# Attention weights exchanged through DRAM instead of turned by TensorE, each pair's reads issued directly behind its own writes

## The reference

```python
def _L1_cond_ref(x, attn_bias, mask, g_in, null_attn_bias, null_kv, Wq, Wkv, Wo, g_out):
    B, N, DIM, H, DH = 8, 256, 256, 16, 64
    xn = layernorm(x, g_in)
    q = (xn @ Wq).reshape(b, n, H, DH).transpose(0, 2, 1, 3) * scale
    k, v = (kv[..., :DH], kv[..., DH:])            # kv = xn @ Wkv, one key head for all 16
    k = jnp.concatenate([nk, k], axis=1)           # one null key ahead of the 256
    v = jnp.concatenate([nv, v], axis=1)
    sim = jnp.einsum('bhid,bjd->bhij', q, k) + bias
    sim = jnp.where(causal_mask, neg, sim)
    sim = jnp.where(mask_p[:, None, None, :], sim, neg)
    attn = jax.nn.softmax(sim, axis=-1)
    out = jnp.einsum('bhij,bjd->bhid', attn, v)
    return layernorm(out.reshape(b, n, INNER) @ Wo, g_out)
```

## Time and profile before

| | |
|---|---|
| median of the runs | 843.15 us (842.95 to 844.2, 3 runs) |
| span of the profiled execution, first to last instruction | 793.7 us |
| what lies around the span, median less span | 49.45 us |
| attention: first transposes of weights to last Wo product | 345.4 to about 657 us of the span |
| PE busy over the span | 748.7 us, 94% |
| DVE / ACT / POOL busy | 453.7 / 381.9 / 422.4 us |

### The profile page before, as it was taken

The page is one execution under the profiler, slowest core; times in us unless marked ns, Lnnn a source line. Parts: engine busy times, 40 slices in busy tenths (PEclk is TensorE's granted clock), DMA queues, the critical chain, the costliest instruction groups (busy, mean ns, idle before and its releaser), DMA issues. The chain is left out here.

```text
span 793.7 us, 16690 instructions
## 1 busy us (share of the span) xinstructions
PE 748.7 (94%) x4993; PEld 595.9 (75%) x4994; DVE 453.7 (57%) x1647; ACT 381.9 (48%) x1094; POOL 422.4 (53%) x506
## 2 busy tenths in 40 slices
PE   8889999769999999989999999999999988899998
PEld 4479966549999999867777777777777754699965
DVE  0824475672232323356666787778878787256557
ACT  3556612242222222166666565656666651777611
POOL 1077327525554852274656668686868356056640
PEclk9999999759999999999999999999999999999999
DMA  9636635429897773395000000000000001356547
GB/s 323 279 108 191 137 118 160 126 81 342 309 329 273 223 231 121 107 401 174 28 1 28 2 28 29 28 29 28 29 1 29 1 29 63 102 160 177 153 149 236
DMA packets 57022, 106.36 MB, mean 134 GB/s; under 512 B 8816, under 2 KB 42864, under 8 KB 55792
## 3 DMA queue, kind: packets, MB, share of 16 engines
q1 hardware_dynamic: 40368, 55.96, 20.9%
q0 software_dynamic: 10944, 30.03, 12.5%
q10 hardware_dynamic: 5632, 19.41, 7.2%
HBM read 78.31 MB, written 27.07 MB: 133 GB/s over the span
## 5 line engine op out<-in xcount | busy, mean ns | idle before, releaser
L2135 POOL TENSOR_TENSOR work<-work,region_ac 128x386 f32<-128x386 f32 x128 | 120.3, 945 | 67.2 <-DVE work L1797 32.7
L1683 ACT ACTIVATE work<-work 128x129 f32<-128x129 f32 (+1 forms) x256 | 114.0, 449 | 5.8 <-DVE work L1797 5.8
L1797 DVE CUSTOM_DVE_ANT_0 work<-psH,work 128x129 f32<-128x129 f32 (+1 forms) x256 | 78.8, 345 | 2.6 <-PE psH L1482 2.6
L1690 ACT COPY work<-psHT 128x384 f32<-128x384 f32 x64 | 30.6, 479 | 86.4 <-PE psHT L1492 86.4
L1355 POOL DMA_INDIRECT d_pairs<-work,home x47 | 46.1, 981 | 42.8 <-DVE home_f L1107 27.4
L1463 PE MATMUL psY<-work,region_ac 128*128 128x256 f32 x256 | 66.9, 384 | 0.5 <-ACT work L1677 0.5
L1516 PE MATMUL psM<-region_ac,work 128*128 128x256 f32 x256 | 66.0, 380 | 0.0
L1025 ACT ACTIVATE work<-work 128x512 f32<-128x512 f32 x39 | 24.6, 630 | 86.0 <-DVE work L1044 86.0
L1344 POOL DMA_INDIRECT b_pairs<-work,home x39 | 38.0, 975 | 49.8 <-DVE work L1051 46.8
L1336 POOL DMA_INDIRECT work<-in_x,inv x39 | 37.0, 949 | 47.0 <-DVE inv L1264 35.5
L848 PE MATMUL psH<-work,region_bd 128*128 128x128 f32 x472 | 59.2, 280 | 2.0 <-ACT region_bd L747 1.1
(11 more groups left out here) (368 smaller groups left out, 1694.6 us busy)
## 6 DMA issues: line engine op xcount, KB each, us to landing
region_bd<-in_b_w ACTq DMA_DIRECT2D x37, 512.0 KB, 5.4
work<-d_rows SPq DMA_DIRECT2D x47, 132.0 KB, 2.2
a_slots<-work SPq DMA_DIRECT2D x19, 256.0 KB, 2.9
region_bd<-in_b_w SPq DMA_DIRECT2D x1, 4096.0 KB, 15.3
work<-b_pairs SPq DMA_DIRECT2D x16, 256.0 KB, 3.1
region_bd<-in_d_w SPq DMA_DIRECT2D x1, 4096.0 KB, 13.2
work<-d_pairs SPq DMA_DIRECT2D x16, 256.0 KB, 4.3
d_rows<-region_bd SPq DMA_DIRECT2D x1, 2112.0 KB, 28.5
```

The source lines that it names most:

```text
L1683: nc.scalar.activation(c_p[:, o, a:z], c_sc[:, o, a:z], ACT.Exp, scale=-1.0, bias=c_min[:, o, i:i + 1], accum_out=c_sum[:, j % 2, o, i:i + ...
L1797: last = nc.vector.tensor_tensor_reduce(c_sc[:, o, a:z], psH[:, o, a:z], c_bm[:, 2 * (j % 2) + o, a:z], 1.0, -LOWEST, ALU.add, ALU.min, c_ ...
L2135: pool.tensor_tensor(c_bm[:, 2 * (j % 2) + o, :], c_mp, c_bias[:, 2 * j + o, :], ALU.subtract).then_inc(C.bm_ready, 1)
```

## The change

PE turns nothing any more. For each pair, DVE turns the weights in 32x32 blocks (`dve_blocks`, one instruction for each head, `c_p` to `c_x1`). SP writes the 384 KB of blocks to a DRAM scratch (`sp_store_blocks`), writes the 4 reciprocals of each partition to another as 512 single elements, and then, in `sp_load_blocks` of the same pair, waits for both writes to land and reads the blocks back in the order in which they make up the turned weights (`c_x2`), and the reciprocals twice, spread over 64 partitions each (`c_over`). SP does this pair after pair in one unrolled loop of 64. The sum of a pair and its product with Wo now come three pairs later (`LAG = 3`) instead of one. `c_x1` and `c_x2` have two slots, `c_over` three, the DRAM scratch four. Scores alternate between the two PSUM tensors `psH` and `psHT`. The keys, the bias and the mask are stored in an order that fits the blocks. `c_x1`, `c_x2`, `c_over` and the values lie where the biases `d_b2` of the last stage were loaded, so these come after the attention; the other weights of the last stage come one piece for each pair from ACT's queue (`act_load_d`), the 4 MB `d_w13` stays on SP ahead of the first pair, and the tiles of `sp_pairs` for later batches are issued by ACT (`act_load_pairs`).

```diff
--- before.py
+++ after.py
...
@@ -26,6 +26,9 @@
 HEADS, DH = 16, 64
 QT = SEQ // P
 KEYS0, KEYS1 = 1 + P, 1 + SEQ
+BLOCK = QT * P + P
+ORDER = (1, 0)
+LAG = 3
 KEYS = KEYS0 + KEYS1
...
         y0_dram = nc.dram_tensor("y0_scratch", [TOKENS, DIM], F32, kind="Internal").ap()
         d_in = nc.dram_tensor("d_rows", [16 * TOKENS, ZROW], F32, kind="Internal").ap()
+        blocks_dram = nc.dram_tensor("c_blocks", [4, 4, P, 2 * BLOCK // 4], F32, kind="Internal").ap()
+        rec_dram = nc.dram_tensor("c_recs", [4, 2 * QT, P], F32, kind="Internal").ap()
 
...
-        def pe_turn(pe, p):
-
-            for o in range(2):
-                pe.wait_ge(C.p_ready, 4 * p + 2 * o + 2)
-                wait(pe, C.pT_ready[o], p)
-                for n, at in enumerate((1, KEYS0 + 1, KEYS0 + 1 + P)):
-                    last = pe.transpose(psHT[:, o, n * P:(n + 1) * P], c_p[:, o, at:at + P], ident[:, :])
-                last.then_inc(C.p_turned, 1)
-
         def pe_sum(pe, p, j, b):
 
-            for s in C.pT_ready:
-                pe.wait_ge(s, p + 1)
+            wait_dma(pe, C.blocks_loaded, 0, p)
             if j == 0:
                 pe.wait_ge(C.v_ready, b + 1)
             wait(pe, C.o_ready, p)
-            for n, keys, queries in ((0, 0, slice(0, SEQ)), (1, 1, slice(P, SEQ))):
-                at = slice(n * SEQ, n * SEQ + queries.stop - queries.start)
+            weights = c_x2[:, p % 2, :, :, :, :].rearrange("p a o i q -> p o i a q")
+            for n, queries, blocks in ((0, slice(0, SEQ), slice(0, QT)), (1, slice(P, SEQ), slice(QT, QT + 1))):
                 for o in range(2):
-                    last = pe.matmul(psL[DH * o:DH * o + DH, queries], c_v[:, keys, :], c_pT[:, o, at],
-                                     start=(n == 0), stop=(n == 1))
+                    last = pe.matmul(psL[DH * o:DH * o + DH, queries].rearrange("p (i a q) -> p i a q", a=4, q=32),
+                                     c_v[:, b % 2, n, :], weights[:, o, blocks, :, :], start=(n == 0), stop=(n == 1))
             last.then_inc(C.pv_mm, 1)
 
...
@@ -1609,12 +1605,11 @@
         def pe_batch(pe, b, odd, first, last):
             for j in range(NPAIR):
                 p = 8 * b + j
-                before = not (first and j == 0)
-                if before:
-                    pe_sum(pe, p - 1, (j - 1) % NPAIR, b - (j == 0))
+                s = p - LAG
                 if not (last and j == NPAIR - 1):
                     pe_scores(pe, p + 1, (j + 1) % NPAIR, b + (j + 1) // NPAIR)
-                pe_turn(pe, p)
+                if s >= 0:
+                    pe_sum(pe, s, s % NPAIR, s // NPAIR)
                 if j == 1 and b >= 3:
                     pe_z_counts(pe, b - 3, psX)
                 if j == 2 and b >= 2:
@@ -1630,9 +1625,10 @@
                 if j == 5 and not last:
                     pe_kv(pe, b + 1, 1 - odd)
                 over = (j + 2) // NPAIR
-                pe_queries(pe, p + 2, (j + 2) % NPAIR, (odd + over) % 2, None if last and over else b + over)
-                if before:
-                    pe_out(pe, p - 1, (j - 1) % NPAIR, b - (j == 0))
+                if not (last and over):
+                    pe_queries(pe, p + 2, (j + 2) % NPAIR, (odd + over) % 2, b + over)
+                if s >= 0:
+                    pe_out(pe, s, s % NPAIR, s // NPAIR)
 
         def batches(eng, batch):
...
-        def act_pT(act, p):
-            act.wait_ge(C.p_turned, 2 * p + 1)
-            wait(act, C.pv_mm, p)
-            nc.scalar.copy(c_pT[:, 0, :], psHT[:, 0, 0:3 * P]).then_inc(C.pT_ready[0], 1)
+        def act_load_d(act, p):
+
+
+            if p < 8:
+                act.dma_start(d_w2[:, 2 * p:2 * p + 2, :], io["d_w2"][:, 2 * p:2 * p + 2, :]).then_inc(D.weights_loaded, 16)
+            elif p < 12:
+                dst, name = ((d_s13, "d_s13"), (d_s2, "d_s2"), (d_sb13, "d_sb13"), (d_b13, "d_b13"))[p - 8]
+                act.dma_start(dst, io[name]).then_inc(D.weights_loaded, 16)
+
+        def act_load_pairs(act, b):
+
+            wait(act, B.combined, 2 * b)
+            for i in range(QT):
+                act.dma_start(c_gat[:, i, :, :], pair_rows(B, 2 * b + i)).then_inc(C.pairs_loaded, 16)
 
         def act_zT(act, b):
...
-        def dve_over(dve, p):
-
-            dve.wait_ge(C.rec_done, p + 1)
-            wait(dve, C.qr_mm, p + 2)
-            nc.vector.tensor_copy(c_over, c_rec.rearrange("p o i -> p i o").unsqueeze(3).to_broadcast([P, QT, 2, DH])
-                                  ).then_inc(C.rec_ready, 1)
...
-        def dve_pT(dve, p):
-            dve.wait_ge(C.p_turned, 2 * p + 2)
-            wait(dve, C.pv_mm, p)
-            nc.vector.tensor_copy(c_pT[:, 1, :], psHT[:, 1, 0:3 * P]).then_inc(C.pT_ready[1], 1)
+            nc.vector.reciprocal(c_rec[:, p % 2, :, :], c_sum[:, j % 2, :, :]).then_inc(C.rec_done, 1)
+
+        def dve_blocks(dve, p, j, o):
+
+
+            n = ORDER.index(o)
+            dve.wait_ge(C.p_ready, 4 * p + 2 * n + 2)
+            if p >= 2 and n == 0:
+                wait_dma(dve, C.blocks_stored, 0, p - 2)
+            nc.vector.transpose(out=c_x1[:, p % 2, :, o, :, :].rearrange("p b i q -> p i b q"),
+                                in_=c_p[:, j % 2, o, 1:1 + BLOCK].rearrange("p (i b q) -> p i b q", b=4, q=32)).then_inc(C.blocks_turned, 1)
 
         def dve_o(dve, p, j):
 
 
             dve.wait_ge(C.pv_mm, p + 1)
-            dve.wait_ge(C.qr_ready, p + 3)
+            wait_dma(dve, C.blocks_loaded, 0, p)
             wait(dve, C.wo_mm, p - 1)
-            nc.vector.tensor_tensor(c_oT[:, j % 2, :], psL[:, 0:SEQ], c_qr[:, j % 2, SEQ:2 * SEQ], ALU.mult).then_inc(C.o_ready, 1)
+            nc.vector.tensor_tensor(c_oT[:, j % 2, :], psL[:, 0:SEQ], c_over[:, p % 3, :], ALU.mult).then_inc(C.o_ready, 1)
 
         def dve_out_raw(dve, b):
...
@@ -2034,46 +2046,43 @@
         def dve_batch(dve, b, odd, first, last):
             for j in range(NPAIR):
                 p = 8 * b + j
+                s = p - LAG
                 more = not (last and j == NPAIR - 1)
-                if not (first and j == 0):
-                    dve_o(dve, p - 1, j + 1)
+                dve_blocks(dve, p, j, ORDER[0])
                 dve_dispatch_start(dve, b, j, last)
                 if j == 0 and not first:
                     dve_v(dve, b)
                 if more:
                     dve_scores_wait(dve, p + 1)
+                    dve_scores(dve, p + 1, j + 1, ORDER[0])
+                dve_blocks(dve, p, j, ORDER[1])
                 dve_sums(dve, p, j)
-                if more:
-                    dve_scores(dve, p + 1, j + 1, 0)
+                if s >= 0:
+                    dve_o(dve, s, s % NPAIR)
+                if j == 3 and not first:
+                    dve_out_raw(dve, b - 1)
                 if j == 6 and not last:
                     dve_k(dve, b + 1)
-                dve_over(dve, p)
-
-                if j == 1 and not first:
-                    dve.wait_ge(C.out_raw, 2 * b)
...
@@ -2277,23 +2289,53 @@
             for i in range(QT):
                 sp.dma_start(c_gat[:, i, :, :], pair_rows(B, 2 * b + i)).then_inc(C.pairs_loaded, 16)
 
-        def sp_load_d(sp):
-
-            sp.wait_ge(fB.y_out, B.NT)
-            for dst, name in ((d_w13, "d_w13"), (d_w2, "d_w2"), (d_s13, "d_s13"), (d_s2, "d_s2"), (d_sb13, "d_sb13"), (d_b13, "d_b13")):
-                sp.dma_start(dst, io[name]).then_inc(D.weights_loaded, 16)
-            load_broadcast(sp, d_b2, "d_b2", D.weights_loaded)
+        def sp_clear_rows(sp):
+
             sp.wait_ge(C.bias_ready, 5)
             first_rows = d_in.rearrange("(e s) n -> e s n", e=16)[:, 0:P, :].rearrange("e p n -> p e n")
-            sp.dma_start(first_rows, stage_zero.unsqueeze(1).to_broadcast([P, 16, ZROW])).then_inc(D.weights_loaded, 16)
+            sp.dma_start(first_rows, stage_zero.unsqueeze(1).to_broadcast([P, 16, ZROW])).then_inc(D.zeroed, 16)
+
+        def sp_store_blocks(sp, p):
+
+
+            r = p % 4
+            sp.wait_ge(C.blocks_turned, 2 * p + 2)
+            if p >= 4:
+                wait_dma(sp, C.blocks_loaded, 0, p - 4)
+            sp.dma_start(blocks_dram[r].rearrange("a (k b) m -> (a k) (b m)", b=4), c_x1[:, p % 2, :, :, :, :].rearrange("p b o i q -> p (b o i q)")
+                         ).then_inc(C.blocks_stored.sems[p % 2], 16)
+            sp.wait_ge(C.rec_done, p + 1)
+            sp.dma_start(rec_dram[r].rearrange("n p -> p n"), c_rec[:, p % 2, :, :].rearrange("p o i -> p (o i)"),
+                         allow_slow_non_contiguous=True).then_inc(C.blocks_stored.sems[p % 2], 16)
+
+        def sp_load_blocks(sp, p):
+
+
+            r = p % 4
+            wait_dma(sp, C.blocks_stored, 0, p)
+            wait(sp, C.pv_mm, p - 1)
+            sp.dma_start(c_x2[:, p % 2, :, :, :, :].rearrange("p a o i q -> p a (o i q)"), blocks_dram[r].rearrange("a s m -> s a m")
+                         ).then_inc(C.blocks_loaded.sems[p % 2], 16)
+            wait(sp, C.o_ready, p - 2)
```

(59 more changed lines are left out.)

151 lines of the change are left out of this document (78 added, 73 removed).

## The result

The changed kernel takes 1292.61 us, the kernel before 843.05 beside it: a ratio of 1.5355, 95% interval 1.5294 to 1.5417. The forecast was 913, range 858 to 1000. The direction was right, the size wrong by a factor of six in the loss.

What follows compares the result with a forecast made beforehand. PE was taken to bound the attention before, SP's serial round trip after: 3.6 + 0.8 + 1.4 = 5.8 us a pair, 70 us more, span 864, with 49.45 around it 913 us; range 858 to 1000.

Steps and rivals of the forecast that it cites:

- What bounded the kernel: Attention before the change: PE alone sets the pace, 4.88 us a pair, of which 0.93 us of transposes would leave PE.
- DVE's exchange: DVE per pair: loses 1.04 us of copy and spreading, gains two block transposes at 0.5 us each, so no change.
- The chain on SP: SP's writes, landing, read issues, then next pair's writes, never overlapping: 5.8 us a pair, chance 0.62 for 4.9 to 7.2.
- The write of blocks: Landing of each pair's 384 KB write to DRAM: 3.6 us, bounds 2.4 and 5.0.
- The tail of the reciprocals: Each pair's 512 elements of 4 bytes, landing behind the blocks: 0.8 us more, between 0.3 and 1.6.
- The rival of slow single elements: Reciprocals' write: at 100 ns per 4 byte write the tail is 3.2 us, period 8.2, total 1061 us; chance 0.13.
- Read issues and wakings: SP's three read issues at 0.37 us, 1.2 us with gaps, and two wakings at 0.1 each: 1.4 us a pair.
- The ends of the stage: Attention's start and end: second pair's write issued at about 357 us, 10 us from the last write to the Wo product's end.
- PE's clock: Rival: PE, 68% busy in the attention, falls to the lower clock; mixed period 6.9 us, total 981 us; chance 0.13.
- The compute's pace: PE and DVE in the attention, if no DMA held them: 4.3 us a pair, between 3.95 and 4.88.
- the quick rival: Writes land within about 3.1 us, so compute sets 4.3 us a pair: 23 us less, 820 us; chance 0.10.
- The 49.45 us around the span: Time outside the profiled span: 793.7 and 49.45 make the median of 843.15; added to the forecast span of 864.

Runs made afterwards that it cites:

- turned_recs: Changed kernel, but DVE also turns the reciprocals in 32x32 blocks and SP writes 16 runs of 128 bytes: period 5.82 us, 915.35 us beside 847.15.

## Why the prediction was wrong

- **What bounded the kernel** was right: PE, at 4.88 us a pair. Of the 0.93 us that left PE nothing showed, as PE no longer sets the pace.
- **DVE's exchange** was about right: a block transpose takes 0.576 us, not 0.5.
- **The chain on SP** was the right mechanism. SP waits for DMA in every pair and hardly ever for DVE, and DVE waits for DMA ahead of its block transposes. The period is less even than I had said, 9.7 to 14.1 us from one write to the next behind the first pair, and the DMA share is 0.47 and 0.35 in the two windows, not well over a half.
- **The write of blocks**: 3.6 assumed, by a choice between 2.4 and 3.9. It takes 3.9 in the mean until the reads are issued, and 4.0 with the second DMA of `turned_recs`; the line through the rows of 128 and 256 KB had given 3.9. The Trainium skill, page DMA: Bandwidth & Descriptors, on the anatomy of one DMA, gives a formula that came to 2.9; the measurement is 1.0 us above it.
- **The tail of the reciprocals** is the step that failed. I took 0.8 us, between 0.3 and 1.6, by packets of 10 to 50 ns. It is 6.1 us (11.90 less 5.75). All rows I had were rates at which an engine works through its packets, and by rate the tail was indeed small: the 4 byte packets took 9 ns each, and the data had moved by 565.7. What lay outside of every row was the time until a write to DRAM is confirmed when eight writes go to the same 32 bytes. By the terms of my sum the measured period divides into 3.9 for the blocks, 6.2 more for the reciprocals (10.1 from write to reads in the mean, less 3.9) and 1.7 for the issues and wakings: 11.8 from the second pair on, where I had 3.6, 0.8 and 1.4.
- **The rival of slow single elements** (0.13, 1061 us) named the right DMA, but by a wrong price and a wrong reason: it gave every element 100 ns, and the same 512 elements cost 0.4 to 0.5 us in all when 32 bytes or more apart. The Trainium skill, page DMA: Bandwidth & Descriptors, section Specifications, speaks of a read, modify and write below 512 bytes. The runs do not contradict it, but the size of a write is not what costs here, its neighbours are. That each write beyond the first waits for the one before is inferred from the steps of 0.6 to 0.8 us; the trace shows only the landing.
- **Read issues and wakings**: 1.4 assumed, 1.67 measured from the issue of the block reads to the next write; the spread reads take 0.59 us each to issue, not 0.37.
- **The ends of the stage** were short too. The second pair's write was issued 37 us behind the first tile of `sp_first_pairs`, not 29, and the last Wo product came 18 us behind the last write, not 10. These 16 us and 62 x (11.79 - 5.8) = 371 are the 387 by which the attention exceeds the 399 that I had forecast.
- **PE's clock** fell, to 0.69 between 500 and 600 us, where I had given that 0.13, and with the clock held up the period was only 0.2 us shorter, since PE was not in the chain. I had priced it as if it were. At the forecast period of 5.8 it holds: `turned_recs` shows clock 1.00 from 500 to 539 us at 5.82 us a pair:

```profile
500.00:539.00 39.00, 28.48 (x186) 18.03 (x186) 28.60 (x122) 16.06 (x64) 21.84 (x29) 1.00 0.55 176
```

- **The compute's pace** of 4.3 was not tested as such. The two kernels in which SP waits for DVE and no longer for its writes run at 4.7, but DVE turns the reciprocals there as well, 0.3 us a pair. At 4.4 to 4.7 (an estimate from these) the quick rival would have ended at 826 to 845 us by my own sum, little or no gain.
- **The 49.45 us around the span** do not exist. A run lies about 2 us above its own span (1300.55 and 1298.5); I had set the span of one chip against the median of another. The error cancels in the difference of the two kernels.
- **The range** was built from the bounds of known rows. For a kind of write that the trace did not hold, its upper bound should have been left far more open.

## What to carry to other kernels

A strided write of single elements to DRAM should be judged by how many of them fall into the same 32 bytes, and turned on chip or spread out first; 2 KB of it cost more here (6.1 us) than the 384 KB beside it (3.9). Where one queue writes, waits and reads back, its period here was the landing plus its issues, whatever double buffers stood around it; issue the reads behind the next writes before counting on an engine's saved time. And where a row gives a rate of packets, it does not bound the time to their landing.

## What the runs showed that I had not expected

- 512 writes of 4 bytes to DRAM: about 0.5 us at 32, 64 or 512 bytes apart against none at all (periods 6.21, 6.24, 6.25 us), 0.65 us more with two in 32 bytes (6.88), 1.8 to 2.2 with four (8.01, 8.46), 5.6 with eight (11.83 to 11.90).
- The landing of such a write, eight to 32 bytes, comes 5.9 us (mean) after the last packet has ended, with the DMA engines idle, and in pieces; without neighbours it is 0.6 to 0.7.
- With two such round trips under way at once, each takes longer (13.4 us from write to reads in place of 10.1).
- DVE turns 128x384 float32 in 32x32 blocks in 0.576 us, and 128x128 in 0.296.
